# Small-head attention: where the mask rows and the shift rows stand against two waits of TensorE

## The chip, the cores and the metric

The kernel runs on one core of a Trainium2 chip. The metric is the device time of one execution in microseconds (us), the median of three runs. The work is spread over TensorE (PE; its weight loads are PEld), VectorE (DVE), ScalarE (ACT), GpSimd (POOL) and SyncE (SP), which run their own instruction streams and meet at semaphores.

## What is computed

A stack of eight residual layers over x of shape (32, 128, 128): a slot-attention stage, product keys, attention blocks, an attention plus experts stage, a recurrent stage, a mixture of experts, six transformer layers and a ternary feed-forward. The change touches the attention with 16 heads of 8 columns each, which two of the stages use. In each of the six layers (NL), first over its own 128 rows, then over the 77 of the context:

```python
def _attn(q, k, v, mask):
    scores = jnp.einsum('bqhd,bkhd->bhqk', q, k) / np.float32(np.sqrt(HD))
    scores = jnp.where(mask[:, None, None, :], jnp.float32(-jnp.inf), scores)
    w = jax.nn.softmax(scores, axis=-1)
    return jnp.einsum('bhqk,bkhd->bqhd', w, v)
...
for i in range(NL):
    ...
    a = _attn(q, k, v, src_mask).reshape(B, L, D) @ so_w[i].T
    ...
    a = _attn(q, k, v, ctx_mask).reshape(B, L, D) @ co_w[i].T
```

The stage of attention plus experts has the same attention with 128 keys and no mask.

## The kernel before

One unit u is one batch row with all of its 16 heads; 32 units make one pass of the attention, and N counts units through the passes of a layer. There are 13 passes: one in the stage of attention plus experts, and in each of six layers one over the row itself ("self", 128 keys) and one over the context ("cross", 77 keys). PSUM has 8 banks of 512 columns. The work of one unit goes around four engines:

- `scores(u)` on PE: the four groups r of four heads have their scores laid in banks 0 to 3, with queries as rows. Where there is a mask, four matmuls of one row each (L179) lay the mask row of the keys first, with `start=True`, and four float32 matmuls of 32 rows (L183, two instructions each) add to them. Group r uses rows 32r to 32r+31 of the array in both.
- `peaks(u)` on DVE: two reductions (L261) find the maxima, the first over banks 0 and 1, which signals `half_peaked`, the second over banks 2 and 3. `split_peaks` writes them in two bfloat16 parts and signals `peaks_ready`.
- `turn_peaks(u)` on PE (L191) and `spread_peaks(u)` on DVE (L274) turn the maxima into `shift`, and signal `shift_ready`.
- `again(u)` on PE: four matmuls of 8 rows (L203) lay the shift rows in banks 0, 1, 4 and 5, again one row group each, and sixteen float32 matmuls (L207) add the scores once more, now with keys as rows.
- `exponential(u, half)` on ACT (L303): half 0 reads banks 0 and 1, half 1 reads banks 4 and 5; both signal `exp_done`.
- `values(u, half)` on PE (L221) multiplies by the values into bank 6, `flatten` on ACT (L311) copies it, `flip(u)` on PE (L229) turns it, `norm(u)` on DVE (L280, L281) divides.

The order on PE is written out by hand in the loop of `small_tensor`: turn_peaks(u), scores(u+1), both halves of values(u-1), a piece of the output projection in the layers (L2615 in even units, L2621 in odd ones), again(u), flip(u-1). A wait in this text holds up all that stands behind it on its engine. The two waits that matter here are in scores(u+1), which waits for half 0 of the exponential of unit u-1 to have read banks 0 and 1 (L175), and in again(u), which waits for `shift_ready` (L195), for `half_peaked` of unit u+1 (its scores in banks 0 and 1 must have been reduced before they are written over, L198) and for the whole exponential of u-1 (L200). Where several waits stand ahead of one instruction, the trace has some of them as instructions of PE's queue of their own (EVENT_SEMAPHORE at L175, L198, L200) and one on the weight load itself.

The recurrent stage appears in the rows only as a place where weight loads have one wait each: L2041 waits for an activation (L2176), L2046 for an operation of DVE (L2095).

Of the kernel before, what the change touches and what calls it, by code (L numbers as in the profile page):

```python
# [29 lines left out]
QUAD = 4  # L30
ROWS = QUAD * HD
# [36 lines left out]
def build(nc, dram, out):  # L68
    with ExitStack() as ctx:
        def sb(name, shape, dt=F32, scope=ctx):  # L70
            return scope.enter_context(nc.sbuf_tensor(name, shape, dt))

        sem = {name: ctx.enter_context(nc.semaphore(name)) for name in SIGNALS}
# [30 lines left out]
        ones_b = sb("ones_b", [128, 128], BF16)  # L104
# [9 lines left out]
        ps = ctx.enter_context(nc.psum_tensor("ps", [128, 8, 512], F32))  # L114
# [41 lines left out]
        AGAIN, SPARE, FLAT, PEAKS = (0, 4), 2, 6, 7  # L156
# [8 lines left out]
        def small_tensor(pe, first, units, keys, q_of, km_of, vt_of, low_of, ready, ready_values, meanwhile=None, area_free=None):  # L165

            rows = lambda r: slice(ROWS * r, ROWS * (r + 1))

            def scores(u):
                N = first + u  # L170
                ready(u)
                if N >= 1:
                    pe.wait_ge(sem["peaks_ready"], N)
                if N >= 2:
                    pe.wait_ge(sem["exp_done"], 2 * N - 3)  # L175
                view = lambda r: ps[:, r, :].rearrange("p (s k) -> p s k", s=QUAD)[:, :, 0:keys]
                if low_of:
                    for r in range(QUAD):
                        nc.tensor.matmul(view(r), ones_b[ROWS * r:ROWS * r + 1, :],  # L179
                                         low_of(u)[ROWS * r:ROWS * r + 1, :].unsqueeze(1).broadcast_to([1, QUAD, keys]),  # L180
                                         start=True, stop=False, skip_group_check=True)
                for r in range(QUAD):
                    last = nc.tensor.matmul(view(r), q_of(u)[rows(r), :], km_of(u)[rows(r), :, :],  # L183
                                            start=(low_of is None), stop=True, skip_group_check=True)
                last.then_inc(sem["scores_done"], 1)
# [7 lines left out]
            def again(u):  # L193

                N = first + u  # L195
                pe.wait_ge(sem["shift_ready"], N + 1)
                if u + 1 < units:
                    pe.wait_ge(sem["half_peaked"], N + 2)  # L198
                if N >= 1:
                    pe.wait_ge(sem["exp_done"], 2 * N)  # L200
                bank = lambda r: AGAIN[r // 2] + r % 2
                for r in range(QUAD):
                    nc.tensor.matmul(ps[0:keys, bank(r), :].rearrange("p (s t) -> p s t", s=QUAD), ones_b[ROWS * r:ROWS * r + 2 * QUAD, 0:keys],  # L203
                                     shift[ROWS * r:ROWS * r + 2 * QUAD, :, :], start=True, stop=False, skip_group_check=True)
                for s in range(QUAD):
                    for r in range(QUAD):
                        last = nc.tensor.matmul(ps[0:keys, bank(r), s * S:(s + 1) * S], km_of(u)[rows(r), s, :],  # L207
                                                q_of(u)[rows(r), :], start=False, stop=True, skip_group_check=True)
                last.then_inc(sem["again_done"], 1)
# [16 lines left out]
            def flip(u):  # L226
# [3 lines left out]
                last.then_inc(sem["o_flipped"], 1)  # L230

            scores(0)
            keep_clock(12, FLAT)
            for u in range(units):
                turn_peaks(u)
                if u + 1 < units:
                    scores(u + 1)
                if u:
                    values(u - 1, 0)
                    values(u - 1, 1)  # L240
                if meanwhile:
                    pe.wait_ge(sem["shift_ready"], first + u + 1)
                    meanwhile(u)
                again(u)
                if u:
                    flip(u - 1)
# [1271 lines left out]
        def stage_attn_experts():  # L1518
            with ExitStack() as st:
# [60 lines left out]
                with nc.Block() as block:  # L1580
# [7 lines left out]
                    def _(pe):  # L1588
# [74 lines left out]
                        def ready_values(u):  # L1663
                            if u % U == 0:
                                pe.wait_ge(sem["spread"], u // U + 1)

                        small_tensor(pe, 0, B, S, lambda u: qr[:, u * S:(u + 1) * S],
                                     lambda u: km[:, (u // U) % 2, :, (u % U) * S:(u % U + 1) * S],
                                     lambda u: vt[:, (u // U) % 2, u % U], None, ready, ready_values)
# [1529 lines left out]
```

## Time and profile before

| | us |
|---|---|
| median of 3 runs | 7483.62 |
| the runs | 7473.76 to 7487.52 |
| profiled execution, whole | 7501.0 |
| its span on the core | 7499.1 |

The profiled execution is one more run beside the three. A timeline row has the start in us from the span's start, the time it took, engine, line, operation, operands and how many instructions were merged in it, and in brackets the idle time of the engine ahead of it and what ended that. "issue" there is idle time for which the profile shows no wait.

### The profile page before, as it was taken

What the parts mean: (1) busy time and instruction counts of PE and PEld (TensorE: products, weight loads), DVE (VectorE), ACT (ScalarE), POOL (GpSimd) and SP (SyncE); (2) the same over time, 40 slices, a digit from 0 to 9 for tenths busy, and PEclk for the clock granted to TensorE, in tenths of its full rate; (3) what the DMA queues carried; (4) which work ended last, traced back from release to release, by engine and by line L of the source; (5) the groups of instructions that cost most, each with busy time, mean ns of one, the idle gap of its engine ahead of it and who ended that gap; (6) DMA issues with size and microseconds to landing.
All of it is one profiled execution on the core that took longest, in us unless ns stands there. A gap on an engine that the chain in (4) does not pass through costs nothing. (4 is left out here: it accounts for less than half of the span.)

```text
span 7499.1 us, 189244 instructions
## 1 busy us (share of the span) xinstructions
PE 5942.4 (79%) x79720; PEld 4358.3 (58%) x79720; DVE 4808.3 (64%) x16917; ACT 2869.8 (38%) x4943; POOL 1029.7 (14%) x924
## 2 busy tenths in 40 slices
PE   4454568898878788888799688888888888888887
PEld 3343446666656577777577456556555565565565
DVE  6777964544558766666544586576675765775864
ACT  2221224444434311111112255456455554554553
POOL 1113522212210200000000110110111111011101
PEclk7667778998989755555699898999999989999988
DMA  1000000000000000000000000000000000000000
GB/s 34 1 0 3 1 30 1 1 1 1 1 5 2 6 3 3 3 3 4 24 1 1 19 2 2 11 2 2 11 2 7 6 2 7 6 2 11 2 2 15
DMA packets 61233, 44.78 MB, mean 6 GB/s; under 512 B 22521, under 2 KB 56125, under 8 KB 60227
## 3 DMA queue, kind: packets, MB, share of 16 engines
q1 hardware_dynamic: 60355, 32.26, 1.6%
q8 instruction: 651, 10.67, 0.6%
q14 instruction: 227, 1.86, 0.1%
HBM read 30.14 MB, written 2.10 MB: 4 GB/s over the span
## 5 line engine op out<-in xcount | busy, mean ns | idle before, releaser
L261 DVE TENSOR_REDUCE peak<-ps 128x8 f32<-128x1024 f32 (+1 forms) x832 | 817.0, 1024 | 261.2 <-PE ps L183 260.4
L303 ACT ACTIVATE e<-ps,H_lowT_c 77x1024 f32<-77x1024 f32 x384 | 405.2, 1104 | 266.4 <-PE ps L207 266.4
L303 ACT ACTIVATE e<-ps,H_lowT_s 128x1024 f32<-128x1024 f32 x384 | 406.7, 1110 | 249.0 <-PE ps L207 249.0
L221 PEld LDWEIGHTS ps<-e,H_vt 128*32 128x32 f32 (+1 forms) x12288 | 323.8, 113 | 259.1 <-ACT e L303 143.2
L221 PE MATMUL ps<-e,H_vt 128*32 128x128 f32 (+1 forms) x12288 | 438.9, 284 | 23.6 <-DVE xs L281 17.7
L2483 POOL TENSOR_TENSOR H_rstd<-H_veps,neghalf 128x4 f32<-128x4 f32 (+1 forms) x146 | 160.8, 1101 | 2123.9 <-DVE H_veps L2479 2123.9
L207 PE MATMUL ps<-H_qr,H_km 32*128 32x128 f32 (+1 forms) x12288 | 430.1, 279 | 0.0
L207 PEld LDWEIGHTS ps<-H_qr,H_km 32*128 32x128 f32 (+1 forms) x12288 | 415.7, 172 | 16.1 <-issue 3.0
L311 ACT ACTIVATE oT<-ps 128x512 f32<-128x512 f32 x416 | 248.4, 597 | 360.3 <-PE ps L221 360.3
L2181 ACT ACTIVATE F_rz<-F_gsum 128x32 f32<-128x32 f32 x256 | 58.6, 229 | 822.8 <-DVE F_gsum L2119 822.8
L183 PE MATMUL ps<-H_km,H_qr 32*128 32x512 f32 (+1 forms) x3072 | 350.8, 524 | 0.0
L280 DVE RECIPROCAL den<-ps 128x16 f32<-128x16 f32 x416 | 107.2, 258 | 320.1 <-PE ps L229 317.2
L274 DVE TENSOR_TENSOR shift<-ps,own_row 128x512 bf16<-128x512 f32 x416 | 283.3, 681 | 18.1 <-PE ps L191 18.1
L229 PE MATMUL ps<-ident,oT 128*128 128x128 f32 x1664 | 281.3, 293 | 4.9 <-ACT oT L311 4.9
L2024 PE MATMUL ps<-F_hp,F_encW 128*128 128x2 f16 x8192 | 253.8, 165 | 36.7 <-issue 34.4
L2024 PEld LDWEIGHTS ps<-F_hp,F_encW 128*128 128x128 f16 x8192 | 238.4, 104 | 37.5 <-issue 37.5
L2050 PE MATMUL ps<-F_eT,F_ctxp 77*128 77x2 f16 x8192 | 253.9, 165 | 0.0
L2301 PEld LDWEIGHTS ps<-G_w,G_hid 128*128 128x128 f32 x2048 | 238.7, 192 | 20.2 <-issue 18.6
L2050 PEld LDWEIGHTS ps<-F_eT,F_ctxp 77*128 77x128 f16 x8192 | 241.2, 104 | 0.0
L2301 PE MATMUL ps<-G_w,G_hid 128*128 128x128 f32 x2048 | 239.0, 275 | 0.0
L2274 PE MATMUL ps<-G_nT,G_w 128*128 128x512 f32 x512 | 233.2, 599 | 0.0
L1231 PE MATMUL ps<-pT,D_vv 77*64 77x128 f32 (+1 forms) x2048 | 164.7, 311 | 84.1 <-ACT pT L1340 54.9
(650 smaller groups left out, 13804.4 us busy)
## 6 DMA issues: line engine op xcount, KB each, us to landing
G_w<-in_L_ffn_w SPq DMA_DIRECT2D x16, 256.0 KB
H_f<-in_L_xcond_f_w SPq DMA_DIRECT2D x12, 256.0 KB
H_nw<-in_L_xcond_n_w SPq DMA_DIRECT2D x21, 128.0 KB, 2.1
A_cond<-in_cond SPq DMA_DIRECT2D x1, 2048.0 KB
out_x<-x_all SPq DMA_DIRECT2D x1, 2048.0 KB, 8.7
ctx_rows<-in_ctx SPq DMA_DIRECT2D x1, 1232.0 KB
D_wq<-in_L_xcond_attn_wq SPq DMA_DIRECT2D x2, 512.0 KB
D_wk<-in_L_xcond_attn_wk SPq DMA_DIRECT2D x2, 512.0 KB
```

What stands on the lines that cost most here:

```text
L183: last = nc.tensor.matmul(view(r), q_of(u)[rows(r), :], km_of(u)[rows(r), :, :], start=(low_of is None), stop=True, skip_group_check=True)
L207: last = nc.tensor.matmul(ps[0:keys, bank(r), s * S:(s + 1) * S], km_of(u)[rows(r), s, :], q_of(u)[rows(r), :], start=False, stop=True, sk ...
L221: last = nc.tensor.matmul(ps[PAD_COLS * s:PAD_COLS * (s + 1), FLAT, r * S:(r + 1) * S], vt_of(u)[0:keys, QUAD * r + s, :], e[0:keys, half, ...
L229: last = nc.tensor.transpose(ps[:, FLAT, r * S:(r + 1) * S], oT[:, r * S:(r + 1) * S], ident[:, :])
L261: last = nc.vector.tensor_reduce(peak[:, HL * half:HL * (half + 1)], view, AX.X, ALU.max, negate=True)
L274: nc.vector.tensor_tensor(shift[:], ps[:, PEAKS, 0:S].unsqueeze(1).broadcast_to([128, QUAD, S]), own_row[:].unsqueeze(2).broadcast_to([128 ...
L303: nc.scalar.activation(e[0:keys, half, :], ps[0:keys, AGAIN[half]:AGAIN[half] + 2, :].rearrange("p b t -> p (b t)"), ACT.Exp, bias=low(u) ...
L311: nc.scalar.activation(oT[:], ps[:, FLAT, :], ACT.Copy).then_inc(sem["o_read"], 1)
L2024: last = nc.tensor.matmul(scored(k)[:, 2 * j:2 * j + 2], encW[:, i, b, :], hp[:, b, :], start=(i == 1 and j == 0), stop=(i == 0), skip_gro ...
L2050: last = nc.tensor.matmul(attended_bank(k)[:, 2 * j:2 * j + 2], ctxp[:, i, CB * c + j, :], eT[:, c, j, :], start=(i == 1 and j == 0), stop ...
L2274: nc.tensor.matmul(ps[:, bank, :], w1[:, x, c * D:(c + 1) * D], nT[:, g % 2, :], start=True, stop=True).then_inc(sem["proj_done"], 1)
L2301: last = nc.tensor.matmul(per(OUT + m % 2)[:, u, :], hid[:, m % 2, c, u * S:(u + 1) * S], w2[:, x, c, :], start=False, stop=(c == 3), skip ...
```

## The change

`lay_low` is a new inner function that lays the mask rows of the groups it is given. In `scores`, the mask rows of groups 2 and 3 (banks 2 and 3) are laid ahead of the wait for the exponential, and those of groups 0 and 1 behind it. In `again`, the shift rows of groups 2 and 3 (banks 4 and 5) are laid first, and the wait for `half_peaked` stands between them and the shift rows of groups 0 and 1. No instruction that computes is added or taken away, and all banks stay as they were.

```diff
+            view = lambda r: ps[:, r, :].rearrange("p (s k) -> p s k", s=QUAD)[:, :, 0:keys]
+
+            def lay_low(u, groups):
+                for r in groups:
+                    nc.tensor.matmul(view(r), ones_b[ROWS * r:ROWS * r + 1, :],
+                                     low_of(u)[ROWS * r:ROWS * r + 1, :].unsqueeze(1).broadcast_to([1, QUAD, keys]),
+                                     start=True, stop=False, skip_group_check=True)
+
             def scores(u):
                 N = first + u
                 ready(u)
                 if N >= 1:
                     pe.wait_ge(sem["peaks_ready"], N)
+                if low_of:
+                    lay_low(u, (2, 3))
                 if N >= 2:
                     pe.wait_ge(sem["exp_done"], 2 * N - 3)
-                view = lambda r: ps[:, r, :].rearrange("p (s k) -> p s k", s=QUAD)[:, :, 0:keys]
                 if low_of:
-                    for r in range(QUAD):
...
+                    lay_low(u, (0, 1))
                 for r in range(QUAD):
                     last = nc.tensor.matmul(view(r), q_of(u)[rows(r), :], km_of(u)[rows(r), :, :],
...
             def again(u):
 
                 N = first + u
+                bank = lambda r: AGAIN[r // 2] + r % 2
                 pe.wait_ge(sem["shift_ready"], N + 1)
-                if u + 1 < units:
-                    pe.wait_ge(sem["half_peaked"], N + 2)
                 if N >= 1:
                     pe.wait_ge(sem["exp_done"], 2 * N)
-                bank = lambda r: AGAIN[r // 2] + r % 2
-                for r in range(QUAD):
+                for r in (2, 3, 0, 1):
+                    if r == 0 and u + 1 < units:
+                        pe.wait_ge(sem["half_peaked"], N + 2)
                     nc.tensor.matmul(ps[0:keys, bank(r), :].rearrange("p (s t) -> p s t", s=QUAD), ones_b[ROWS * r:ROWS * r + 2 * QUAD, 0:keys],
                                      shift[ROWS * r:ROWS * r + 2 * QUAD, :, :], start=True, stop=False, skip_group_check=True)
```

In the order of the instructions a row is a run of equal ones, a matmul with its weight load, and the waits that stand ahead of the first. PE in a self pass, before, from one turn of the maxima to the next:

```order
L191 MATMUL ps<-ident_b,peak_parts 128x128 [waits peaks_ready]
L179 MATMUL ps<-H_low_s,ones_b 128x512 [waits exp_done,peaks_ready]
L179 MATMUL ps<-H_low_s,ones_b 128x512 x3
L183 MATMUL ps<-H_km,H_qr 128x512 x4
L221 MATMUL ps<-e,H_vt 32x128 [waits o_normed,exp_done]
L221 MATMUL ps<-e,H_vt 32x128 x7
```

The same place in the changed kernel, where L173 is the mask row and L189 the scores:

```order
L197 MATMUL ps<-ident_b,peak_parts 128x128 [waits peaks_ready]
L173 MATMUL ps<-H_low_s,ones_b 128x512 [waits peaks_ready]
L173 MATMUL ps<-H_low_s,ones_b 128x512
L173 MATMUL ps<-H_low_s,ones_b 128x512 [waits exp_done]
L173 MATMUL ps<-H_low_s,ones_b 128x512
L189 MATMUL ps<-H_km,H_qr 128x512 x4
```

Two of the four mask rows now stand ahead of the wait for `exp_done`, and that wait, which shared an instruction with `peaks_ready`, is now the only one of its instruction. PE at `again` in the pass without a mask, before:

```order
L203 MATMUL ps<-shift,ones_b 128x512 [waits exp_done,half_peaked,shift_ready]
L203 MATMUL ps<-shift,ones_b 128x512 x3
L207 MATMUL ps<-E_qr,E_km 128x128 x16
```

And changed, where L209 is the shift row:

```order
L209 MATMUL ps<-shift,ones_b 128x512 [waits exp_done,shift_ready]
L209 MATMUL ps<-shift,ones_b 128x512
L209 MATMUL ps<-shift,ones_b 128x512 [waits half_peaked]
L209 MATMUL ps<-shift,ones_b 128x512
```

The three waits of one instruction are now two and one.

## Rows read from the trace of the kernel before

**Rows 1.** Waits: engine, line, waited for: us in total, times, longest

```profile
PE ps L179 <- ACT e L303: 241.4, 360, 1.1
```

**Rows 2.** Timeline of a self pass in layer 2: an odd, then an even unit

```profile
5422.08 2.12 ACT L303 ACTIVATE e<-ps,H_lowT_s 128x1024 f32<-128x1024 f32 x2 [0.79 <-PE ps L207]
...
5424.66 2.36 DVE L261 TENSOR_REDUCE peak<-ps 128x8 f32<-128x1024 f32 x2 [0.84 <-PE ps L183]
5425.54 0.71 PE L2621 MATMUL ps<-H_so_w,H_o8T 128*128 128x128 f32 x4
...
5426.18 0.40 PE L203 MATMUL ps<-shift,ones_b 8*128 8x512 bf16 x4
...
5427.55 2.12 ACT L303 ACTIVATE e<-ps,H_lowT_s 128x1024 f32<-128x1024 f32 x2 [1.27 <-PE ps L207]
...
5428.77 0.13 PEld L179 LDWEIGHTS ps<-H_low_s,ones_b 1*128 1x128 bf16 x4 [0.80 <-issue]
5428.81 0.40 PE L179 MATMUL ps<-H_low_s,ones_b 1*128 1x512 bf16 x4 [0.67 <-ACT e L303]
...
5429.02 1.04 PE L183 MATMUL ps<-H_km,H_qr 32*128 32x512 f32 x8
...
5429.99 1.08 PE L221 MATMUL ps<-e,H_vt 128*32 128x128 f32 x32
5430.13 2.36 DVE L261 TENSOR_REDUCE peak<-ps 128x8 f32<-128x1024 f32 x2 [0.62 <-PE ps L183]
...
5431.42 0.13 PEld L203 LDWEIGHTS ps<-shift,ones_b 8*128 8x128 bf16 x4 [0.22 <-issue]
...
5432.81 2.12 ACT L303 ACTIVATE e<-ps,H_lowT_s 128x1024 f32<-128x1024 f32 x2 [0.80 <-PE ps L207]
```

**Rows 3.** Short timelines: half 0 of the exponential alone, self, then cross with its release

```profile
5427.55 1.11 ACT L303 ACTIVATE e<-ps,H_lowT_s 128x1024 f32<-128x1024 f32 x1 [1.27 <-PE ps L207]
...
5601.06 1.11 ACT L303 ACTIVATE e<-ps,H_lowT_c 77x1024 f32<-77x1024 f32 x1 [1.28 <-PE ps L207]
...
5602.28 0.09 PEld L179 LDWEIGHTS ps<-H_low_c,ones_b 1*128 1x128 bf16 x1 [0.89 <-issue]
```

**Rows 4.** Line L175: durations in ns (least, median, most) of its waits

```profile
L175 PEldq EVENT_SEMAPHORE  x402: 51/51/51, 2331.7 to 7274.6; - x134
```

**Rows 5.** Short timelines of the recurrent stage: two releases of a weight load

```profile
3003.69 0.32 ACT L2176 ACTIVATE F_ex<-ps,F_nm 16x77 f32<-16x77 f32 x1 [0.15 <-DVE F_nm L2087]
...
3004.06 0.20 PEld L2041 LDWEIGHTS ps<-ident,F_ex 16*77 16x77 f32 x1 [0.42 <-ACT F_ex L2176]
...
3004.61 0.17 DVE L2095 SCALAR_TENSOR_TENSOR F_eT<-ps,F_eT 77x16 f16<-77x16 f32 x1
...
3004.84 0.10 PEld L2046 LDWEIGHTS ps<-F_eT,F_ones 77*128 77x128 f16 x1 [0.30 <-DVE F_eT L2095]
```

**Rows 6.** Short timeline of the pass without a mask: first reduction, then shift rows

```profile
2428.88 1.23 DVE L261 TENSOR_REDUCE peak<-ps 128x8 f32<-128x1024 f32 x1 [0.62 <-PE ps L183]
...
2430.18 0.13 PEld L203 LDWEIGHTS ps<-shift,ones_b 8*128 8x128 bf16 x4 [0.61 <-issue]
```

**Rows 7.** Timeline of a cross pass: values, first reduction alone, shift rows

```profile
5603.08 1.08 PE L221 MATMUL ps<-e,H_vt 77*32 77x128 f32 x32
...
5603.21 0.80 DVE L261 TENSOR_REDUCE peak<-ps 128x8 f32<-128x616 f32 x1 [0.36 <-PE ps L183]
...
5604.46 0.12 PEld L203 LDWEIGHTS ps<-shift,ones_b 8*77 8x77 bf16 x4 [0.17 <-issue]
```

**Rows 8.** Windows: stretch, busy us (instructions) of PE, PEld, DVE, ACT, POOL, granted clock

```profile
4495.00:4545.00 50.00, 43.76 (x553) 29.82 (x554) 24.63 (x59) 20.35 (x28) 0.71 (x2) 0.56 0.01 2
...
5027.00:5077.00 50.00, 40.00 (x752) 28.23 (x750) 31.81 (x76) 26.02 (x35) 1.00 (x2) 0.86 0.01 2
...
7110.00:7160.00 50.00, 43.76 (x571) 30.23 (x571) 25.11 (x60) 20.42 (x28) 1.18 (x3) 0.59 0.01 2
...
5031.00:5187.00 156.00, 132.81 (x2696) 94.93 (x2696) 107.05 (x287) 99.39 (x134) 9.46 (x12) 0.96 0.01 3
```

More of the change, by code:

```diff
@@ L173, in scores @@
                     pe.wait_ge(sem["peaks_ready"], N)
+                if low_of:
+                    lay_low(u, (2, 3))
                 if N >= 2:
                     pe.wait_ge(sem["exp_done"], 2 * N - 3)
-                view = lambda r: ps[:, r, :].rearrange("p (s k) -> p s k", s=QUAD)[:, :, 0:keys]
                 if low_of:
-                    for r in range(QUAD):
-                        nc.tensor.matmul(view(r), ones_b[ROWS * r:ROWS * r + 1, :],
-                                         low_of(u)[ROWS * r:ROWS * r + 1, :].unsqueeze(1).broadcast_to([1, QUAD, keys]),
-                                         start=True, stop=False, skip_group_check=True)
+                    lay_low(u, (0, 1))
                 for r in range(QUAD):
```

## The prediction, made before the changed kernel ran

> **What bounds the kernel now.** I looked first at the waits of TensorE, since the change only moves its instructions past two waits. One of them stands out: the mask rows of the next unit wait for the exponential 360 times, 241.4 us in all [rows 1]. That is every unit of the twelve masked passes except the first two of each (384 less 24). Whether this wait lies on the path is read from the timeline of a self pass [rows 2], followed around once. Half 0 of the exponential starts at 5427.55 and takes 1.11 [rows 3]; the mask rows' weights load at 5428.77, the scores L183 start at 5429.02, the values L221 at 5429.99, the shift rows' weights load at 5431.42, and the next exponential starts at 5432.81. So the period of this even unit is 5432.81 - 5427.55 = 5.26 us, that of the odd unit ahead of it 5427.55 - 5422.08 = 5.47 us, and it is one chain: ACT, PE, (DVE), PE, ACT. Every 0.01 us taken from the step "exponential ends, mask rows start" shortens the period, until something else is late.
>
> The second wait, for the first half of the next maxima, is late only in some units. In the even unit DVE starts its reductions at 5430.13 and 2.36 us for two puts the end of the first near 5431.34; the shift rows follow at 5431.42, so DVE decides [rows 2]. In the odd unit the first reduction ends near 5424.66 + 1.2 = 5425.9, while PE is in L2621 until the shift rows start at 5426.18: PE decides [rows 2]. In a cross pass the reduction ends at 5603.21 + 0.80 = 5604.01 and the shift rows start only at 5604.46: PE decides in every unit [rows 7]. In the pass without a mask DVE decides in every unit: 2428.88 + 1.23 = 2430.11 against 2430.18 [rows 6].
>
> **What moving the rows themselves brings: next to nothing.** One would think that two of four matmuls leave the stretch behind the wait. But the four run side by side: the four mask rows together take 0.40 us from first start to last end, and the scores start 5429.02 - 5428.81 = 0.21 us behind the first [rows 2], which is one pass of 512 columns at the full clock of 2.4 GHz. The four groups use different row groups of the array. Two such matmuls take the same 0.21 us as four, and the first of L183 belongs to group 0, whose mask row still starts behind the wait. What is left is the distance at which the matmuls start one after another. I take it as 0 to 0.01 us: a gain of at most 360 x 0.01 = 3.6 us. In `again` group 0 moves from first place to third, which delays the first L207 by as much where PE decides, in about 290 of 416 units: a loss of at most 2.9 us. I take the two together as nothing.
>
> The Trainium skill has the same picture as a rule (TensorE: Matmul & The Clock Gate, section on packing small matmuls): matmuls on different row groups overlap, and each further one adds about 4 ns. By that page the two that leave would be worth 8 ns, an estimate of 360 x 0.008 = 2.9 us. It speaks against a gain from the moved rows; the trace agrees, with 0.21 us for four.
>
> **What the move does to the waits: the term that counts.** The order shows that the first mask row had two waits, `exp_done` and `peaks_ready`. The trace has one of them as an instruction of its own at L175, 51 ns each time, least and most alike, 402 times [rows 4]. This piece stands between the exponential and the first weight load. From its end to that load the self unit takes 5428.77 - (5427.55 + 1.11) = 0.11 us [rows 2, 3], the cross unit 5602.28 - (5601.06 + 1.11) = 0.11 us [rows 3]. In the changed kernel `exp_done` is the only wait of its matmul. What such a release takes is seen in the recurrent stage, where ACT ends at 3003.69 + 0.32 = 3004.01 and the weights load at 3004.06: 0.05 us [rows 5]. So each of the 360 waits that end late is shorter by 0.11 - 0.05 = 0.06 us. **360 x 0.06 = 21.6 us.** The bounds: 0.05 if only the 51 ns go (18.0 us), 0.07 with the rounding of the rows (25.2 us). The pass without a mask keeps both waits on one instruction and gains nothing here.
>
> For the shift rows the same holds in small. `half_peaked` shared one instruction with two others, and the release took 2430.18 - 2430.11 = 0.07 us [rows 6]; alone it should take what L2046 takes behind DVE, 3004.84 - (3004.61 + 0.17) = 0.06 us or, with the rounding, 0.05 us [rows 5]. That is 0.02 us in the 31 units of the pass without a mask and in the even units of six self passes, some 84 behind the start of each: 115 x 0.02 = 2.3 us. The bound below is 0.
>
> **Does something else become late?** In the self unit DVE is idle 0.62 us ahead of its reductions, waiting for PE, and ACT 0.80 us and more ahead of the exponential [rows 2]. The values of the cross pass start at 5603.08 for half 0; half 1 is needed half of the 1.08 us later, near 5603.5 by the weight loads, and half 1 of the exponential ends near 5601.06 + 2.1 = 5603.17 [rows 3, 7]. There is at least 0.2 us of slack on each, so 0.08 us passes through to the period. No DMA stands in this loop. The mask rows laid early write banks 2 and 3 while ACT reads banks 0 and 1; PE already writes one bank while others are read in the same units (values into bank 6 during the reductions), at no price that shows.
>
> **The sum.** 21.6 + 2.3 + 0 = 23.9 us. The profiled execution took 7501.0, so it would take 7477.1. The runs before have a median of 7483.62, 17 us under the profiled one; the same 23.9 us from the median gives **7459.7 us**.
>
> **The rivals.**
>
> *The release is no shorter* (0.13). If a weight load with its own wait behind two in flight costs as much as the separate instruction did, only start distances are left, 0 to 3 us: 7481 to 7484. For it: no weight load of the trace has exactly this neighbourhood. Against it: the 0.05 us of [rows 5].
>
> *The rows that move are worth half of their pass* (0.05). Then each late mask wait gains a further 0.10 us (36 us) and each of the 115 units in which DVE decides 0.10 us (12 us): 7459.7 - 48 = 7412. Against it: 0.21 us for four.
>
> *The clock of the cross passes* (0.12 for faster, 0.05 for slower). In the first 50 us of a cross pass the granted clock is 0.56 to 0.59 in three of the six layers and 0.86 in the other three; the first and last of the three at 0.56 to 0.59 and one at 0.86 are shown [rows 8]. That is 2.4 GHz falling to 1.2 GHz for most of that stretch. At the lower clock PE gets through 553 to 571 instructions instead of 752; at the pace of a whole cross pass, 2696 in 156 us or 17.3 per us [rows 8], that is some (752 - 571) / 17.3 = 10.5 us per layer. The change shifts where each pass lies and puts more PE work into its waits, so each of the six starts is drawn anew. If all three start at 0.86 instead: 31 us less in the profiled execution, and some 15 us less against the median, since its runs seem to have had one or two low starts fewer (7501.0 - 7483.6 = 17 us, an estimate): 7445. The case on the other side is this mechanism too: it ends slower than before once three more starts than in the median run go to the lower clock, 3 x 10.5 = 31.5 us against 23.9. With all six low the time is 7477.1 + 31.5 = 7508.6 us, 25 us over the median before. For it: the clock differs between layers that do the same work. Against it: six equal draws.
>
> *Nothing but a part of it* (0.10): one or two more low starts, or a period that gives back half in units I did not follow: 7470 to 7480.
>
> **The numbers.** The forecast, 7459.7 with 7450 to 7468 around it, has 0.55. What a measurement of this kernel can tell from no change is 0.2%, 15 us, so the faster side ends at 7468.7. Faster: 0.55 + 0.12 + 0.05 = 0.72, and 0.01 from the last case, 0.73. Within 0.2%: 0.13 and most of the last case, 0.21. Slower: 0.06. The range for 8 in 10 takes in the forecast, most of the case of the better clock and the partial one, and most of "no shorter": 7440 to 7482.
>
> **What would show it.** In the changed trace, the distance from the end of half 0 of the exponential to the weight load of the third mask row (L173) must be 0.05 us, and the scores must still start 0.21 us behind it: the first says where the gain is, the second that the moved rows brought none. There must be no EVENT_SEMAPHORE at the line of that wait except in the pass without a mask. The periods should be 5.18 and 5.41 us in self passes (5.26 and 5.47 before by the same rows) and 0.06 us less in cross passes. If the distance is still 0.11 us, the main step is wrong. If the periods shrink by 0.1 us and more, the rows do not run side by side as I read them. If the periods are as said and the time is not, the windows of the cross passes will have another clock.

## The result, and the profile after

The changed kernel takes 7424.37 us (median of five runs, 7415.48 to 7438.0) against 7483.62 (five runs, 7473.76 to 7487.52). The ratio is 0.9925, with a 95% interval of 0.9911 to 0.994: 59 us faster, where 24 us were forecast, and below the range of 7440 to 7482. The profiled execution took 7424.37 us, its span is 7422.5 us.

The waits of the changed kernel (engine, tile, line, waited for: us in total, times, longest), and its EVENT_SEMAPHORE instructions at the two lines of waits in `scores`: L181 is `peaks_ready`, L185 is `exp_done`.

```profile
PEld ps L173 <- ACT e L309: 208.9, 359, 1.0
```

```profile
L181 PEldq EVENT_SEMAPHORE  x90: 51/51/51, 4281.2 to 7185.3; - x90
```

```profile
L185 PEldq EVENT_SEMAPHORE  x30: 51/51/51, 2320.3 to 2465.7; - x30
```

Against [rows 4], the 402 separate instructions have become 120. The 30 at L185 belong to the pass without a mask, which keeps its two waits on one instruction. In the twelve masked passes none is left behind the exponential. The 90 at L181 stand ahead of the early mask rows, where PE has time.

The timeline of a self pass after, an even then an odd unit (start, time it took, engine, line; in brackets the idle time ahead and what ended it); it answers to [rows 2]:

```profile
5400.89 2.12 ACT L309 ACTIVATE e<-ps,H_lowT_s 128x1024 f32<-128x1024 f32 x2 [1.28 <-PE ps L213]
...
5401.42 0.39 PE L173 MATMUL ps<-H_low_s,ones_b 1*128 1x512 bf16 x2
...
5402.05 0.09 PEld L173 LDWEIGHTS ps<-H_low_s,ones_b 1*128 1x128 bf16 x2 [0.55 <-ACT e L309]
5402.06 0.39 PE L173 MATMUL ps<-H_low_s,ones_b 1*128 1x512 bf16 x2 [0.25 <-ACT e L309]
...
5402.07 1.23 PE L189 MATMUL ps<-H_km,H_qr 32*128 32x512 f32 x8
...
5403.23 1.08 PE L227 MATMUL ps<-e,H_vt 128*32 128x128 f32 x32
5403.39 2.36 DVE L267 TENSOR_REDUCE peak<-ps 128x8 f32<-128x1024 f32 x2 [0.53 <-PE ps L189]
...
5404.61 0.15 PEld L209 LDWEIGHTS ps<-shift,ones_b 8*128 8x128 bf16 x4 [0.17 <-issue]
...
5406.04 2.12 ACT L309 ACTIVATE e<-ps,H_lowT_s 128x1024 f32<-128x1024 f32 x2 [0.78 <-PE ps L213]
...
5411.41 1.11 ACT L309 ACTIVATE e<-ps,H_lowT_s 128x1024 f32<-128x1024 f32 x1 [1.28 <-PE ps L213]
```

The periods are 5406.04 - 5400.89 = 5.15 us and 5411.41 - 5406.04 = 5.37 us, 10.52 for the pair; before it was 5.26 + 5.47 = 10.73. The forecast pair was 10.59.

A cross pass, the exponentials of before and then those of after with the values' weights behind the first:

```profile
5601.06 2.11 ACT L303 ACTIVATE e<-ps,H_lowT_c 77x1024 f32<-77x1024 f32 x2 [1.28 <-PE ps L207]
5605.83 2.11 ACT L303 ACTIVATE e<-ps,H_lowT_c 77x1024 f32<-77x1024 f32 x2 [0.73 <-PE ps L207]
5610.87 2.11 ACT L303 ACTIVATE e<-ps,H_lowT_c 77x1024 f32<-77x1024 f32 x2 [1.27 <-PE ps L207]
```

```profile
5561.16 2.11 ACT L309 ACTIVATE e<-ps,H_lowT_c 77x1024 f32<-77x1024 f32 x2 [1.28 <-PE ps L213]
...
5563.08 0.81 PEld L227 LDWEIGHTS ps<-e,H_vt 77*32 77x32 f32 x32 [0.42 <-issue]
...
5565.84 2.11 ACT L309 ACTIVATE e<-ps,H_lowT_c 77x1024 f32<-77x1024 f32 x2 [0.73 <-PE ps L213]
...
5570.79 2.11 ACT L309 ACTIVATE e<-ps,H_lowT_c 77x1024 f32<-77x1024 f32 x2 [1.28 <-PE ps L213]
```

The pair falls from 4.77 + 5.04 = 9.81 to 4.68 + 4.95 = 9.63 us. Twelve passes of 31 periods, 15.5 pairs each, give 6 x 15.5 x (0.21 + 0.18) = 36 us, and one more comes from the pass without a mask: **some 37 us of steady gain**.

The other part is the clock. Windows of the first 50 us of a cross pass in the changed kernel, the first and the last layer (columns as in [rows 8]; the granted clock is the figure behind POOL's):

```profile
4477.00:4527.00 50.00, 43.08 (x760) 29.26 (x762) 32.34 (x79) 27.54 (x37) 0.62 (x2) 0.86 0.01 2
...
7051.00:7101.00 50.00, 43.09 (x760) 28.90 (x759) 32.16 (x77) 27.95 (x37) 0.61 (x1) 0.86 0.01 2
```

All six layers stand at 0.86, where [rows 8] had three of six at 0.56 to 0.59. In both kernels the clock drops to 1.2 GHz at the start of every cross pass. How long it stays there is worked out from the windows, which hold only full and half clock: a share of 0.86 over 50 us is 0.14 x 50 x 2 = 14 us at half clock, 0.90 is 10 us, 0.59 is 41 and 0.56 is 44 us. I call the last two a long fall.

### The profile page after: what moved, and what is told of

Its sections match the earlier page's. It is cut to its first block and busy times, and to the rows that moved or that the text cites. A ratio compares the mean times of both kernels' runs of the same rounds, so it can differ in the third digit from the quotient of the medians.

```text
span 7422.5 us, 188919 instructions
## 1 busy us (share of the span) xinstructions
PE 6016.0 (81%) x79720; PEld 4349.7 (59%) x79720; DVE 4805.5 (65%) x16917; ACT 2871.0 (39%) x4943; POOL 1030.7 (14%) x924
## 5 line engine op out<-in xcount | busy, mean ns | idle before, releaser
L227 PE MATMUL ps<-e,H_vt 128*32 128x128 f32 (+1 forms) x12288 | 429.4, 280 | 23.9 <-DVE xs L287 17.7
L189 PE MATMUL ps<-H_km,H_qr 32*128 32x512 f32 (+1 forms) x3072 | 401.1, 543 | 0.0
```

What stands on the lines that cost most here:

```text
L227: last = nc.tensor.matmul(ps[PAD_COLS * s:PAD_COLS * (s + 1), FLAT, r * S:(r + 1) * S], vt_of(u)[0:keys, QUAD * r + s, :], e[0:keys, half, ...
```

## Experiments

Three things had to be told apart: the shape of the waits, the moved rows themselves, and the clock at the start of a pass. For each kernel I read the time from the end of half 0 of the exponential to the weights of the values behind it, "the way" below, because it holds every step of the mask rows and the scores. Before it is 1.33 us in self and 0.91 us in cross passes, after 1.23 and 0.81 us (5403.23 - 5402.00, and 5563.08 - 5562.27). Medians are compared with runs of the kernel before made in the same session: 7490.07 for the first four, 7483.43 for the next four, 7481.73 for the last four. Within these three sessions the runs of the kernel before (9 to 23 of them) spread over 27 to 65 us and those of the others (4 to 12) over 6 to 33, for reasons that come below.

### Each half of the change alone

The `scores` part of the diff alone, `again` as before:

> Only the part in scores: two mask rows ahead of the wait, again as in the kernel before. Measure: the time from the end of half 0 of the exponential to the first weight load of the values of a self pass, 1.33 us before, 1.23 us changed. If nearly all of the gain in the attention is here: 1.23 us, and 360 units x 0.10 = 36 us under the kernel before without any difference in the clock, some 7425 to 7447 us. If the part in again carries half of it: 1.28 us and 18 us. If the low clock at the start of cross passes goes away because of the mask rows that run during the wait, all six first stretches of 50 us have a granted clock of 0.86; if it is a draw, two to four of the six.

```profile
5399.16 2.12 ACT L309 ACTIVATE e<-ps,H_lowT_s 128x1024 f32<-128x1024 f32 x2 [0.81 <-PE ps L213]
...
5400.33 0.09 PEld L173 LDWEIGHTS ps<-H_low_s,ones_b 1*128 1x128 bf16 x2 [0.57 <-ACT e L309]
...
5404.53 2.12 ACT L309 ACTIVATE e<-ps,H_lowT_s 128x1024 f32<-128x1024 f32 x2 [1.27 <-PE ps L213]
...
5409.72 2.12 ACT L309 ACTIVATE e<-ps,H_lowT_s 128x1024 f32<-128x1024 f32 x2 [0.82 <-PE ps L213]
```

7440.39 us (7436.1 to 7449.24), ratio 0.9937 [0.9916, 0.9958]. The rows are the timeline of its self pass: periods of 5.37 and 5.19 us, 10.56 for the pair, and the way has its full cut, 1.23 and 0.81 us. Nearly all of the steady gain is here. No cross pass had a long fall (0.90 in all six windows).

The `again` part alone, `scores` as before:

> Only the part in again: shift rows of groups 2 and 3 ahead of the wait for the maxima. The release of the mask rows stays at 0.11 us and the way to the values at 1.33 us. If the part in again is small: periods shorter by 0.03 us in the pass without a mask and in even self units, nothing in cross passes, 2 to 4 us in all, no verdict from the times except by the clock. If groups run ahead on their own (the first matmuls of the second scores start before the last shift rows have ended) it could be 0.05 us and more per unit, 20 us. Clock: if shift rows in a wait keep it up, fewer low starts than three of six.

```profile
5405.45 2.12 ACT L303 ACTIVATE e<-ps,H_lowT_s 128x1024 f32<-128x1024 f32 x2 [1.28 <-PE ps L207]
...
5406.68 0.13 PEld L179 LDWEIGHTS ps<-H_low_s,ones_b 1*128 1x128 bf16 x4 [0.81 <-issue]
...
5410.68 2.12 ACT L303 ACTIVATE e<-ps,H_lowT_s 128x1024 f32<-128x1024 f32 x2 [0.76 <-PE ps L207]
```

7460.09 us (7453.46 to 7468.58), ratio 0.9962 [0.995, 0.9975]. By the medians over all units, the even self unit has 5.23 us instead of 5.26, the odd one and the cross units some 0.007 us more, and a unit of the pass without a mask has 0.03 less: a steady gain of 2 us. The median is 30 us under that of before. It had no long fall either (0.86 in all six windows). So a part worth 2 us by its own loop carries 28 us of something else.

### The wait without the rows, and the rows without the wait

Here no row moves; in units behind the first, `scores` no longer repeats the wait for `peaks_ready`, which `turn_peaks` has met just ahead of it:

```diff
-                if N >= 1:
+                if N >= 1 and u == 0:
                     pe.wait_ge(sem["peaks_ready"], N)
```

> The kernel before without the repeated wait for peaks_ready in scores, which turn_peaks has already made; all four mask rows stay behind the exponential. So exp_done is the only wait of its matmul and no row moves. The step of the prediction that counted: the release falls from 0.11 to 0.05 us in 360 masked units and also in some 30 units of the pass without a mask, 390 x 0.06 = 23 us; the way from the exponential to the values falls from 1.33 to 1.27 us. If the shape of the wait is worth nothing: 0 us. If it is all of the gain in the attention: 1.23 us. Clock: no work is added in the wait, so if such work is what keeps the clock up, two to four of six cross passes still start at 0.56 to 0.59; if the shorter period is enough, none.

```profile
5400.75 2.12 ACT L303 ACTIVATE e<-ps,H_lowT_s 128x1024 f32<-128x1024 f32 x2 [0.81 <-PE ps L207]
...
5401.92 0.10 PEld L179 LDWEIGHTS ps<-H_low_s,ones_b 1*128 1x128 bf16 x4 [0.82 <-ACT e L303]
5401.92 0.39 PE L179 MATMUL ps<-H_low_s,ones_b 1*128 1x512 bf16 x4 [0.59 <-ACT e L303]
...
5402.15 1.03 PE L183 MATMUL ps<-H_km,H_qr 32*128 32x512 f32 x8
```

```profile
L175 PEldq EVENT_SEMAPHORE  x97: 51/51/51, 2338.5 to 7216.6; - x97
```

7444.21 us (7430.72 to 7457.04), ratio 0.9935 [0.9913, 0.9957]. With all four mask rows behind the wait the way is 1.24 and 0.82 us in three units of four. The rows show where: half 0 ends at 5400.75 + 1.11 = 5401.86, the weights load at 5401.92 and the matmul starts at 5401.92 with them. In [rows 2] the load stood 0.11 us behind the end of the exponential and the matmul another 0.04 us behind the load. So one wait instead of two saves 0.15 - 0.06 = **0.09 us**, not the 0.06 that the load alone shows. (By the medians over the late units: load 0.114 and matmul 0.144 us behind before, 0.051 and 0.055 here.) The pass without a mask, which the prediction left out, gains too here: its period is 4.96 us against 5.04 in 23 of 30 units, and the pass is 1.9 us shorter. Two of the six cross passes had a long fall (0.59), so the single wait alone does not rule them out.

The row of L175 shows what this kernel does not get rid of: 97 separate instructions are left. In about one unit of four `ready(u)` waits for the operands of a new group, and then two waits meet at the mask row again and the way is 1.33 and 0.91 us (82 units of the masked passes). In the changed kernel those waits too stand ahead of the early rows. This is the one thing that moving the rows buys: 82 x 0.09 = 7 us.

The opposite: two rows ahead as in the change, and `peaks_ready` repeated ahead of the other two, so that the two waits meet at the third row (`again` as before):

```diff
+                if low_of:
+                    lay_low(u, (2, 3))
                 if N >= 2:
+                    pe.wait_ge(sem["peaks_ready"], N)
                     pe.wait_ge(sem["exp_done"], 2 * N - 3)
```

> Two mask rows ahead of the wait as in the changed kernel, but the wait for peaks_ready is repeated behind them, so that exp_done shares its matmul with a second wait as in the kernel before. The release stays at 0.11 us. If moved rows are worth what the prediction said: the way to the values is 1.33 or 1.32 us, 0 to 4 us. If they are worth the rest of what the changed kernel shows: 1.29 us, 360 x 0.04 = 14 us. Clock: if the work in the wait keeps it up, six of six cross passes start at 0.86.

```profile
5399.91 2.12 ACT L310 ACTIVATE e<-ps,H_lowT_s 128x1024 f32<-128x1024 f32 x2 [1.27 <-PE ps L214]
```

```profile
5401.14 0.12 PEld L173 LDWEIGHTS ps<-H_low_s,ones_b 1*128 1x128 bf16 x2 [0.62 <-issue]
5401.17 0.39 PE L173 MATMUL ps<-H_low_s,ones_b 1*128 1x512 bf16 x2 [0.35 <-ACT e L310]
```

7475.09 us (7462.94 to 7495.96), ratio 0.9984 [0.9969, 0.9998]. The load stands 0.12 us and the matmul 0.15 us behind the end of the exponential, as before the change. The way is 1.323 and 0.904 us against 1.330 and 0.911 (medians): two matmuls fewer behind the wait are worth 0.007 us. The 4 ns per packed matmul that the Trainium skill gives (TensorE: Matmul & The Clock Gate, section on packing small matmuls) would make that 8 ns, and here the trace agrees.

The loop explains 360 x 0.007 = 2.5 us of the 15 us between the medians. All six windows stand at 0.86, as the expectation had it for work in the wait, but the runs reach 7495.96 us at a mean clock of 0.837, so that other executions seem to have had long falls. A third term, of 10 us, is read below from the recurrent stage.

Then both at once, more work and no less of it behind: rows 2 and 3 are laid ahead and once more behind the same two waits, so their matmuls are done twice and the output is the same.

> The mask rows of groups 2 and 3 are laid ahead of the wait and once more behind it, with the waits of the kernel before (exp_done shares its matmul with peaks_ready). So nothing moves off the path; PE only has two more matmuls in the wait. Way from the exponential to the values: 1.33 us as before, at most 0.02 less. If work in the wait is what keeps the clock up at the start of cross passes: none of six starts at 0.56 to 0.59, and the time is below the kernel before by what those starts cost, 10 to 30 us. If the clock there is a draw that goes by where the passes lie: two to four low starts and a time within 10 us of the kernel before.

```profile
5401.43 2.12 ACT L310 ACTIVATE e<-ps,H_lowT_s 128x1024 f32<-128x1024 f32 x2 [1.27 <-PE ps L214]
...
5402.65 0.13 PEld L173 LDWEIGHTS ps<-H_low_s,ones_b 1*128 1x128 bf16 x4 [0.62 <-issue]
```

```profile
4471.00:4521.00 50.00, 45.13 (x575) 30.58 (x576) 24.23 (x57) 20.44 (x28) 0.61 (x1) 0.56 0.01 2
5002.00:5052.00 50.00, 42.24 (x768) 29.20 (x766) 31.26 (x75) 26.22 (x36) 0.61 (x1) 0.86 0.01 2
```

7461.42 us (7450.63 to 7474.61), ratio 0.9969 [0.9953, 0.9985]. The release is 0.11 us again and no period differs from before by more than 0.002 us, and yet the median is 22 us lower. The windows show one long fall in six (the first; the other five are like the second row). Work in the wait of each unit makes nothing in the loop faster, and does not rule the falls out. Some 13 of the 22 us lie in the recurrent stage, which comes below.

### Both kernels again, and the clock

The same two kernels, unchanged, for a second profile of each:

> The kernel before, unchanged, for a second profile. If low starts go by layers that lie at certain places: again in layers 0, 3 and 5. If they are drawn anew in each execution: one to four, in other layers. Periods 5.46 and 5.26 us in self passes, 5.04 and 4.77 in cross passes.

> The changed kernel, unchanged, for a second profile. If work in the waits keeps the clock up, no low start in six cross passes; if it was a lucky draw, two to four. Periods 5.37 and 5.15 us in self passes, 4.95 and 4.68 in cross passes.

```profile
4488.00:4538.00 50.00, 43.76 (x565) 29.85 (x566) 24.39 (x58) 20.43 (x28) 0.61 (x1) 0.56 0.01 2
5020.00:5070.00 50.00, 43.76 (x552) 29.81 (x553) 24.65 (x58) 20.26 (x28) 0.80 (x2) 0.56 0.01 2
5553.00:5603.00 50.00, 39.75 (x748) 27.84 (x745) 31.19 (x75) 26.85 (x36) 0.61 (x1) 0.86 0.01 2
```

The windows are those of the kernel before: five of its six cross passes had a long fall (all but the third row's), and the execution took 7527.45 us, 26 us more than the first profile with three. The changed kernel took 7422.44 us and had none (0.86 to 0.90). From the first exponential of one self pass to that of the next layer the kernel before takes 519.0 to 519.3 us where the cross pass between has the short fall (523.1 once, in the second profile), and 528.7 to 532.5 with a long one: **10 to 13 us for each long fall**. The 23 executions beside the first four experiments say it too: the fastest took 7467.88 us at a mean clock of 0.844, the slowest 7520.27 at 0.834, and the time rises as the clock falls in between.

The profiles hold a further difference, outside the attention. The recurrent stage is a loop of four rounds, in code that no kernel here touches, and its clock is 0.50 in all of them. From one activation L2176 to the next it takes 4.1 us, but at the three turns of the loop 16.2, 17.0 and 17.5 us in the kernel before. PE behind the first turn, in the kernel before and in the one with the gap filled, which follows:

```profile
2828.71 0.99 PE L2024 MATMUL ps<-F_hp,F_encW 128*128 128x2 f16 x32 [10.75 <-issue]
```

```profile
2824.91 1.01 PE L2024 MATMUL ps<-F_hp,F_encW 128*128 128x2 f16 x32 [7.14 <-issue]
```

PE stands idle without a wait that the profile shows, 10.75 us or 7.14. The three turns together take 50.6 and 51.2 us in the two profiles of the kernel before, 47.8 and 48.8 in those of the changed one, 47.9, 49.7 and 46.9 with scores alone, again alone and the wait alone, 40.3 with the rows alone and 37.8 with more work. They go by the kernel and hardly by the execution. Why is open: the code of the stage is the same, only the instructions ahead of and behind it differ. So 10 us of what the rows-only kernel gains, and 13 of what the one with more work gains, are this, and neither the attention's loop nor its clock.

Twice the clock-keeping matmuls in the kernel before (L162, which run behind the first scores of each pass):

```diff
-            keep_clock(12, FLAT)
+            keep_clock(24, FLAT)
```

> The kernel before with 24 instead of 12 extra matmuls behind the first scores of each pass, meant to hold the clock. They cost PE some 12 x 0.11 us more in each of 13 passes, 13 to 17 us, if nothing hides them. If low starts come from too little work at the start of a pass: none of six, and the time is some 0 to 15 us below the kernel before. If not: low starts stay at two to four and the time is 10 to 20 us above it.

7460.58 us (7442.23 to 7474.46), ratio 0.9966 [0.9949, 0.9982], with two long falls in six cross passes. That is 23 us better than before, but the turns of the recurrent loop take 37.8 us here, 13 us less, so the matmuls themselves bought some 10. The falls are still there, short ones in all the other cross passes. The first turn of the maxima in a cross pass shows why:

```profile
4993.99 0.23 PE L191 MATMUL ps<-ident_b,peak_parts 128*128 128x128 bf16 x1 [1.79 <-DVE peak_parts L269]
```

The kernel before at the same place, with PE at the start of a cross pass and the window there:

```profile
5026.80 1.48 PE L162 MATMUL ps<-ones_b 128*128 128x256 bf16 x12
5031.39 0.29 PE L191 MATMUL ps<-ident_b,peak_parts 128*128 128x128 bf16 x1 [3.11 <-DVE peak_parts L269]
```

```profile
5030.00:5040.00 10.00, 6.38 (x78) 3.93 (x82) 5.07 (x11) 2.99 (x4) 0.00 (x0) 0.53 0.01 2
```

The twelve matmuls end at 5028.28, PE waits 3.11 us for the first split of the maxima, and the clock is at half just then. With 24 it still waits 1.79 us. So the gap was to be filled: 40 in place of 12, in an otherwise unchanged kernel before.

> The kernel before with 40 instead of 12 of the keep_clock matmuls behind the first scores of each attention pass. In the kernel before PE is idle for 3.1 us there (L162 ends, the first turn of the maxima waits for DVE), and the clock then goes to half for 12 us or for 42 us. 28 more at 0.12 us each are 3.4 us and fill the gap. By the theory that this gap decides the clock of the start: no cross pass falls to half at all, the window of the first 50 us stands at 0.95 or more in all six, and the time falls by the long falls of the median run (two or three at 10.5 us) and the short ones: 7435 to 7455. By the rival, that the fall comes from the lower activity of the pass's first units or from chance: the falls stay, between one and five of them long, the extra matmuls run at half clock and hold up the first turn by some 3 us in such passes, and the time is 7470 to 7500.

```profile
4479.12 4.54 PE L162 MATMUL ps<-ones_b 128*128 128x256 bf16 x40
4483.71 0.23 PE L191 MATMUL ps<-ident_b,peak_parts 128*128 128x128 bf16 x1
```

```profile
4478.00:4528.00 50.00, 41.50 (x835) 30.07 (x839) 34.79 (x81) 28.73 (x39) 2.32 (x3) 1.00 0.01 3
```

7413.88 us (7408.97 to 7421.71), ratio 0.9908 [0.9893, 0.9923]: 68 us faster, better than the change itself and than the 7435 to 7455 that I expected. The first turn follows the last keeping matmul with hardly a gap, and all six windows stand at 1.00, with some 790 instructions of PE beside the keeping ones where the short fall lets 740 through. The periods are those of before. From layer to layer it takes 511.9 to 512.1 us, 7 us less than the kernel before without a long fall: the short falls were not free either. Five layers are steady to 0.2 us now, and the five runs spread over 13 us where nine of before spread over 27. Not all of the 68 us are the clock: the turns of the recurrent loop take 37.6 us, 13 us less than before, so some 55 are, 42 of them the 7 us of six layers and the rest the long falls (an estimate). With the gap open, at some 3.1 us or at 1.8, the clock fell in every cross pass, and closed in none. So the gap ahead of the first turn decides whether it falls there.

The changed kernel with none of these matmuls:

> The changed kernel without the 12 keep_clock matmuls. It had no long fall of the clock in 12 starts of cross passes in two profiles. If that rests on how much PE does around the gap, taking 1.5 us of work away brings long falls back: two or more of six starts at a granted clock under 0.6 in their first 50 us, and 7445 or more. If it rests on the faster units behind the start, whose busy share is higher, the starts stay at 0.86 or so and the time stays within 7 us of 7424.

```profile
6528.00:6578.00 50.00, 41.91 (x746) 28.42 (x746) 32.34 (x79) 27.13 (x37) 1.04 (x2) 0.86 0.01 2
7041.00:7091.00 50.00, 45.17 (x566) 30.69 (x567) 24.33 (x58) 20.58 (x29) 0.61 (x1) 0.56 0.01 2
```

7419.02 us (7414.09 to 7428.29), ratio 0.991 [0.9893, 0.9926]. One long fall in six, against none in twelve with 12 matmuls, and the time is within 6 us of the changed kernel (the turns of the recurrent loop take 46.0 us, some 2 less). It lies between the two expectations: the changed loop meets a long fall more seldom than the old one, but is not safe from it, and 12 matmuls, which leave the gap open, are worth next to nothing.

### A better version

The changed kernel with the single wait in the pass without a mask as well, and with the plain order of `again` in cross passes:

```diff
-                if N >= 1:
+                if N >= 1 and (low_of or u == 0):
                     pe.wait_ge(sem["peaks_ready"], N)
...
-                for r in (2, 3, 0, 1):
-                    if r == 0 and u + 1 < units:
+                ahead = keys == S
+                if not ahead and u + 1 < units:
+                    pe.wait_ge(sem["half_peaked"], N + 2)
+                for r in (2, 3, 0, 1) if ahead else range(QUAD):
+                    if ahead and r == 0 and u + 1 < units:
```

> The changed kernel with two things more. In the pass without a mask, scores(u) for u of 1 and up no longer repeats the wait for peaks_ready (turn_peaks(u-1), ahead of it on PE, waited for the same value), so its weight load has the one wait for the exponential. And the split order in again is kept for passes of 128 keys, while the cross passes have the plain order with half_peaked first. By the theory that a wait alone on its weight load saves 0.09 us: the period of the pass without a mask falls from 5.01 to 4.92 us, 31 x 0.09 = 2.8 us; the cross units get back the 0.008 us that the split order cost them, 6 x 31 x 0.008 = 1.5 us; together 4 us, about 7420, and the time from the end of the exponential to the values stays at 1.23 and 0.81 us. By the rival, that most of this kernel's lead over its own sum is the clock at the start of the cross passes, drawn anew with every shift of the program: the same periods, but one or more of the six starts at a granted clock under 0.6 in their first 50 us, and 10 us more for each, 7430 to 7450.

```profile
2402.01 1.94 ACT L312 ACTIVATE e<-ps 128x1024 f32<-128x1024 f32 x2 [1.04 <-PE ps L216]
2403.08 0.31 PEld L189 LDWEIGHTS ps<-E_km,E_qr 32*128 32x128 f32 x8 [0.75 <-ACT e L312]
...
2406.94 1.94 ACT L312 ACTIVATE e<-ps 128x1024 f32<-128x1024 f32 x2 [1.04 <-PE ps L216]
```

7403.36 us (7399.07 to 7405.3), ratio 0.989 [0.9874, 0.9907]. The period without a mask is 4.93 us, as the rows show, against 5.01 in the changed kernel, but in 23 of 30 units only, and the pass is 1.9 us shorter; cross units gain some 0.006 us each, at most 1 us. It is 21 us under the changed kernel, though, where 4 were expected. Its layers take 511.6 to 512.1 us, those of the changed kernel 515.0 to 515.6 in most (over both profiles), and the difference lies in stretches at half clock again: 6.8 us at the start of self passes instead of 10.2, and 17.1 behind the cross passes instead of 20.5. My expectation, that the clock would at best stay the same, was wrong.

The same with the gap filled, 40 matmuls for 12:

> The last but one kernel (the changed kernel with the single wait in the pass without a mask and the plain order in again of cross passes) with 40 instead of 12 keep_clock matmuls. If the gap ahead of the first turn decides the clock at the start: no half clock at the start of the cross passes, where the changed kernel still has 12 us of it in each, and 3 to 5 us less in each of six: 7395 to 7405. If it does not: the same falls, the extra matmuls at half clock in each: 7425 to 7440.

```profile
4465.00:4515.00 50.00, 45.13 (x864) 31.73 (x868) 35.94 (x85) 29.63 (x40) 2.03 (x3) 1.00 0.01 3
```

**7367.44 us** (7363.81 to 7376.98), ratio 0.9847 [0.9832, 0.9862]: 114 us under the kernel before and some 57 under the change. Five of six windows are at 1.00 and one at 0.97. The layers take 505.0 to 506.0 us. Here too the expectation (7395 to 7405) was too careful, by 28 us and more: self passes lose their half clock at the start as well, and the stretch behind the cross pass has 13.7 us of it in place of 17.1. Some 8 us more are again the turns of the recurrent loop, 37.9 us here against 46.2 without the 28 matmuls.

## Why the prediction was wrong

**Right:** the place, the chain of a unit, and which wait mattered. `scores` brought nearly all of the steady gain. The release to the weights is 5402.05 - 5402.00 = 0.05 us as forecast; no EVENT_SEMAPHORE is left there outside the pass without a mask. Nothing else became late: 0.10 us taken from the way shortens the self pair by 0.21 and the cross pair by 0.18.

**The step that failed** is the term of the sum "each of the 360 waits that end late is shorter by 0.11 - 0.05 = 0.06 us". It measured up to the weight load. But the matmul is what the scores wait for, and it too comes closer: in [rows 2] it starts 0.04 us behind its load at 5428.77, in the changed kernel at 5402.06 against 5402.05. From the end of the exponential to the matmul it is 0.15 us before and 0.06 after, 0.144 and 0.054 by the medians, so 360 x 0.09 = 32 us for the 21.6 put down. The bounds, 0.05 to 0.07, were bounds of the same wrong end of the interval. The wait-only kernel measures the term without the moved rows. The numbers to see it were in [rows 2]. By itself this term would have made the forecast some 7449, which is still outside what was measured: the other 25 us are the clock and what stays open below.

**"What moving the rows themselves brings: next to nothing"** held for the array: 0.007 us. With the 0.09 of the wait it makes the 0.10 by which the way is shorter. The sign that the prediction gave, that periods shorter by 0.1 us and more mean that the rows do not run side by side, was a wrong one: the periods of 5.26 and 5.47 us did shrink by 0.11 and 0.10, and it was the wait. One detail was read wrongly: the scores were to start 0.21 us behind the third mask row, and they start 0.01 behind it, at 5402.07. Those are most likely the groups whose rows were laid early. It brings nothing, since all eight take 1.23 us instead of 1.04 and end as late as before. A second effect was missed: the early rows also take the waits of `ready(u)` off the instruction behind the exponential, in 82 units, 7 us that the sum held already, as it counted all 360.

**The shift rows** gave 0.03 us in the even self units and in the pass without a mask, where 0.02 was forecast, and cost some 0.007 in the others: 2 us in all, as forecast.

**The rival "the clock of the cross passes"**, put at 0.12 on the faster side, came true on top of the forecast, not in its stead. The price of 10.5 us per low start was a little small (10 to 13), and "six equal draws" was wrong as an argument against it: the kernel before had long falls in 8 of 12 starts over two profiles, the changed one in none of 12. The forecast ought to have let the two cases add up. With its own 23.9 us and one and a half long falls it would have said 7483.6 - 23.9 - 18 = 7442, with the loop as measured 7483.6 - 37 - 18 = 7429. The range was also said to take in most of "no shorter", and took in 7481 to 7482 of its 7481 to 7484.

**What stays open.** The budget from median to median is 37 us of loop, and 18 to 24 for the one and a half to two long falls of a median run of before (an estimate, from the clock and time of its runs). Against that the changed kernel has more half clock at the start of self passes and behind cross passes, some 2 us per layer, 12 us. That makes 43 to 49 of 59 us, and the turns of the recurrent loop add 2 to 3. Some 7 to 14 us are not placed. When the first attention pass starts differs by 11 us between the first two profiles, in code that no kernel here touches, but by 1 us the other way between the second two, so it belongs to the execution. And what decides between a short and a long fall, once PE has had its gap, was not found. It isn't the faster release (two long falls in six with it alone). With rows laid in a wait and 12 keeping matmuls, the profiles have one long fall in 42 starts (the changed kernel twice, scores alone, again alone, rows alone, more work, the better version); without such rows they have 12 in 24 (before twice, wait alone, 24 keeping matmuls). That speaks for the work in the waits, but does not show it: the starts of one execution are not independent, each kernel has one or two profiles, and other executions of two of these kernels took longer at a lower clock than the profiled one (7495.96 us at 0.837 against 7469.71 at 0.841 with the rows alone, 7474.61 at 0.842 against 7456.2 at 0.847 with more work), so they seem to have had more long falls (an estimate). Only filling the gap is shown to end both kinds, up to one window at 0.97.

## What to carry to other kernels

Where a wait ends late on PE's path, let it be the only wait of its instruction: leave out waits already met, or put a cheap independent instruction ahead to carry them; and measure from the releaser's end to the start of the matmul, not to the weight load. Look at each place where PE idles a few us at the start of a stage, and fill it up to the instruction that ends the idling: half filled it bought some 10 us here, filled some 55. When runs of one kernel spread wider than those of its variants, a term that is drawn anew in each run is in the times, and a forecast has to add it to its sum. And before a difference of medians is put down to a change, compare the two profiles in the stages that the change does not touch: here up to 13 us lay in one of them.

## What the hardware showed that I had not expected

- A second wait in front of a weight load costs more than the 51 ns of its own instruction: 0.09 us from releaser to matmul, since behind it the matmul trails its load by 0.03 to 0.04 us instead of starting within 0.01.
- A gap of 3.1 us between L162 and L191 goes with 14 us or with 41 to 44 us at 1.2 GHz, in the same code from layer to layer; the pass with the long one is 10.7 us longer. With a gap of 1.8 us the falls are still there, without the gap there is none. The Trainium skill (TensorE: Matmul & The Clock Gate, section on oscillation in real kernels) tells of a kernel whose clock fell in its waits for DMA and came back behind them, and advises a loop that keeps PE busy; the gap-filled kernel agrees, with 1.00 in all six windows.
- The clock couples distant places: stretches at half clock behind the cross pass changed between 13.7, 17.1 and 20.5 us in kernels whose code there is the same.
- Three turns of one and the same loop, in the recurrent stage, took 50.6 and 51.2 us in one kernel and 37.6 in another that differs only in 28 matmuls per attention pass elsewhere.
